# Macaron block on one core: value products of two ticks in one burst, a third buffer of probabilities, bias parts inside the room of y, new plan targets

## The reference, cut to what matters

```python
def ffn(x):                      # on layernormed x
    x_prev = shift_down_by_one_token(x)
    xr = mu_r * x + (1 - mu_r) * x_prev
    xk = mu_k * x + (1 - mu_k) * x_prev
    return sigmoid(xr @ W_r.T) * (square(relu(xk @ W_k.T)) @ W_v.T)

def attn(x):                     # on layernormed x, 16 heads of 16
    q, k, v = split(x @ W_qkv + b_qkv)
    q, k = rope(q), rope(k)
    p = softmax(causal(q @ k.T / 4))
    return (p @ v) @ W_proj + b_proj

x = x + 0.5 * ffn(layernorm(x))
x = x + attn(layernorm(x))
x = x + 0.5 * ffn(layernorm(x))
```

## Time and profile before

| | |
|---|---|
| median of three executions | 3384.6 us |
| profiled execution | 3389.39 us, of which the span 3387.7 us |
| TensorE busy | 3108.6 us (92%) |
| VectorE busy | 2535.7 us (75%) |
| ScalarE busy | 2154.7 us (64%) |
| GpSimd busy | 1488.3 us (44%) |
| mean granted TensorE clock | 0.967 |

### The profile page before, as it was taken

One profiled execution on the slowest core, in us unless ns is written; L12 is line 12 of the kernel. 1 busy time (PEld: TensorE's weight loads), 2 busy tenths in 40 slices (PEclk: granted clock), 3 DMA queues, 4 the chain that ended last, 5 costly groups with the idle time before them and its releaser, 6 DMA issues.

```text
span 3387.7 us, 57478 instructions
## 1 busy us (share of the span) xinstructions
PE 3108.6 (92%) x18368; PEld 1649.0 (49%) x18368; DVE 2535.7 (75%) x8449; ACT 2154.7 (64%) x4737; POOL 1488.3 (44%) x2135
## 2 busy tenths in 40 slices
PE   5689999999899999999999899999999999998997
PEld 4433545545454554545545454554545455454434
DVE  3678888787777877778787777887778787777762
ACT  3266666666666666666666666666666666666663
POOL 5333444454444444454454444444354444444322
PEclk9799999999999999999999999999999999999997
DMA  2334342442433425343442433434343442433321
GB/s 84 49 70 77 67 83 68 76 85 56 91 71 67 87 55 94 67 80 67 76 89 52 92 69 70 82 61 94 62 83 68 76 89 52 89 71 68 70 55 35
DMA packets 201143, 245.36 MB, mean 72 GB/s; under 512 B 67845, under 2 KB 102025, under 8 KB 200841
## 3 DMA queue, kind: packets, MB, share of 16 engines
q1 hardware_dynamic: 200840, 241.69, 36.0%
HBM read 53.35 MB, written 51.38 MB: 31 GB/s over the span
## 4 chain that ended last, share of the span: by engine, by line
PE 66%; DVE 9%; ACT 7%; SPq 6%; DMA 5%; issue 4%; POOL 4%; POOLq 0%; ACTq 0%; DVEq 0%
PE ps_y L597 14%; PE ps_s L575 12%; PE ps_m L582 11%; PE ps_d L654 6%; PE ps_d L648 6%; PE ps_d L642 5%; PE ps_d L645 5%; DMA sw_sb<-qb_sb 4%; DVE ps_m L777 4%; SPq L525 4%; PE ps_d L632 3%; ACT pt_sb L683 3%; PE ps_d L658 2%; PE ps_d L604 2%; DVE ka_sb L801 1%
## 5 line engine op out<-in xcount | busy, mean ns | idle before, releaser
L683 ACT ACTIVATE pt_sb<-ps_s 128x512 f32<-128x512 f32 (+3 forms) x3072 | 1481.5, 494 | 1075.0 <-PE ps_s L575 1058.3
L777 DVE CUSTOM_DVE_ANT_0 ps_m<-ps_m,mask_sb 128x512 f32<-128x512 f32 (+3 forms) x3072 | 1692.5, 568 | 588.8 <-PE ps_m L582 575.7
L582 PE MATMUL ps_m<-kr_sb,qr_sb 96*128 96x512 bf16 (+3 forms) x3072 | 1009.0, 331 | 92.5 <-DVE mx_sb L777 73.6
L575 PE MATMUL ps_s<-qr_sb,kr_sb 99*128 99x512 bf16 (+3 forms) x3072 | 1013.9, 334 | 42.1 <-ACT pt_sb L683 34.8
L902 POOL TENSOR_SCALAR_AFFINE_SELECT pt_sb<-pt_sb 128x512 f32<-128x512 f32 x512 | 343.4, 671 | 949.0 <-ACT pt_sb L683 949.0
L575 PEld LDWEIGHTS ps_s<-qr_sb,kr_sb 99*128 99x128 bf16 x3072 | 299.0, 98 | 838.3 <-issue 324.9
L597 PE MATMUL ps_y<-pt_sb,v_sb 128*32 128x512 f32 (+3 forms) x6144 | 672.7, 510 | 0.0
L777 DVE DVE_READ_ACCUMULATOR2_ANT mx_sb<- 128x1 f32 x3072 | 433.6, 141 | 0.0
L582 PEld LDWEIGHTS ps_m<-kr_sb,qr_sb 96*128 96x128 bf16 x3072 | 300.2, 98 | 215.7 <-DVE mx_sb L777 64.0
L654 PE MATMUL ps_d<-axn_sb,wqk_sb 128*128 128x256 f32 x1024 | 305.5, 392 | 25.2 <-DVE dif_sb L813 23.5
L642 PE MATMUL ps_d<-ka_sb,wk_sb 128*128 128x256 f32 x1024 | 306.0, 396 | 21.7 <-DVE ka_sb L801 20.1
(11 more groups left out here) (74 smaller groups left out, 3215.0 us busy)
## 6 DMA issues: line engine op xcount, KB each, us to landing
kr_sb<-part_sb SPq DMA_DIRECT2D x384, 128.0 KB, 4.5
qr_sb<-part_sb SPq DMA_DIRECT2D x384, 128.0 KB, 4.8
sw_sb<-qb_sb SPq DMA_DIRECT2D x512, 64.0 KB, 2.0
y_way<-yt_sb SPq DMA_DIRECT2D x128, 256.0 KB, 2.2
x_sb<-x SPq DMA_DIRECT2D x64, 256.0 KB, 2.9
yn_sb<-y_way SPq DMA_DIRECT2D x64, 256.0 KB
den_sb<-r_way SPq DMA_DIRECT2D x64, 256.0 KB
out<-x_sb SPq DMA_DIRECT2D x64, 256.0 KB, 2.2
```

Source lines behind the costliest of these rows:

```text
L575: eng.matmul(ps_s[:, slot % NS, 0:width], kr_sb[0:KR + NP, n % RS, j, kb * P:(kb + 1) * P], qr_sb[0:KR + NP, n % RS, j, q0:q0 + width], st ...
L582: eng.matmul(ps_m[:, u % NM, 0:width], qr_sb[0:KR, n % RS, j, i * P:(i + 1) * P], kr_sb[0:KR, n % RS, j, piece * QC:piece * QC + width], s ...
L683: eng.activation(pt_sb[:, tick % 2, j, 0:width], ps_s[:, slot % NS, 0:width], ACT.Exp, scale=SCALE).then_inc(exped, 1)
L777: eng.tensor_tensor_reduce(ps_m[:, u % NM, 0:width], ps_m[:, u % NM, 0:width], mask_sb[:, m0:m0 + width], 1.0, -3e38, ALU.add, ALU.max, mx ...
```

## The change

Five things are edited.

1. `pv` now takes a pair of ticks: first all waits of both ticks, then the 16 MATMUL instructions of both. It runs once in 8 slots, at `slot % 8 == 2` (`PV_AT` 3 becomes 2), for the pair that ended 3 slots before. Before, it ran each 4 slots, for the tick that ended 4 slots before. `pved` counts pairs now, and every wait on it is converted.
2. `pt_sb` has three buffers (`PT = 3`). The third takes 8 KB a partition.
3. `bp_sb` and `bparts_sb` lie inside `yt_sb`; `y_copy` waits once for the bias to be split and sent.
4. The plan's targets. Second feed-forward of batches up to nb-3: base 92 + 25c becomes 70 + 24c. First feed-forward from batch 2 on: -20 + 15c becomes -44 + 18c. Attention's layernorm: 2 + 16c becomes -10 + 18c. `r_QK` of the first pair: 8 + 16c becomes -4 + 18c. `a_V` and `a_bv`: 60 slots behind the layernorm's target becomes 100.
5. With `PV_AT` the y steps' target `done` moves one slot forward.

```diff
--- before.py
+++ after.py
@@ -42,7 +42,8 @@
 NTK = len(TICKS)
 GSLOTS = NTK * G
 BSLOTS = NG * GSLOTS
-PV_AT = 3
+PV_AT = 2
+PT = 3
 MAX_ORDER = [i for k in range(TT // 2) for i in (TT - 1 - k, k)]
 UNITS = [(i, j, piece) for i in MAX_ORDER for j in range(G) for piece in range(i // KQ + 1)]
 NU = len(UNITS)
@@ -86,12 +87,12 @@
                 return at + 160 + 8 * c
             if b == self.nb - 2:
                 return at + BSLOTS + 16 + 24 * c
-            return at + BSLOTS + 92 + 25 * c
+            return at + BSLOTS + 70 + 24 * c
         if b == 0:
             return FIRST + 5 * c
         if b == 1:
             return -60 + 20 * c
-        return at - BSLOTS - 20 + 15 * c
+        return at - BSLOTS - 44 + 18 * c
 
     def describe(self):
         nb, s = self.nb, self.step
@@ -126,7 +127,7 @@
         for b in range(nb):
             for c in range(NCH):
                 i = b * NCH + c
-                t = FIRST + 24 + 6 * c if b == 0 else (b - 1) * BSLOTS + 2 + 16 * c
+                t = FIRST + 24 + 6 * c if b == 0 else (b - 1) * BSLOTS - 10 + 18 * c
                 s("DVE", "a_st0", i, 0.33, t, ("f_xadd", self.ffn_at[b, c, 0], 2), ("a_st1", i - 1, 0))
                 s("DVE", "a_st1", i, 0.51, t, ("a_st0", i, 0), ("a_x1", i - 1, 1))
                 s("POOL", "a_rstd", i, 1.3, t, ("a_st1", i, 3), ("a_x1", i - 1, 1))
@@ -134,15 +135,15 @@
                 s("ACT", "a_x1", i, 0.36, t, ("a_x0", i, 0))
                 s("PE", "a_T", i, 0.5, t, ("a_x1", i, 2))
                 s("ACT", "a_xn", i, 0.48, t, ("a_T", i, 1), ("a_V", i - NCH, 1), ("r_QK", (b - 1) * 2 * NCH + NCH + c, 1))
-                s("PE", "a_V", i, 4, t + 60, ("a_xn", i, 2))
-                s("DVE", "a_bv", i, 0.67, t + 60, ("a_V", i, 1))
+                s("PE", "a_V", i, 4, t + 100, ("a_xn", i, 2))
+                s("DVE", "a_bv", i, 0.67, t + 100, ("a_V", i, 1))
             for pair in range(2):
                 for c in range(NCH):
                     i = (2 * b + pair) * NCH + c
                     if b == 0:
                         t = -40 + 18 * c if pair else FIRST + 32 + 6 * c
                     else:
-                        t = (b - 1) * BSLOTS + (104 + 22 * c if pair else 8 + 16 * c)
+                        t = (b - 1) * BSLOTS + (104 + 22 * c if pair else -4 + 18 * c)
                     s("PE", "r_QK", i, 4, t, ("a_xn", b * NCH + c, 2))
                     s("ACT", "r_b0", i, 0.36, t, ("r_QK", i, 1), ("r_low", i - 2, 1))
                     s("ACT", "r_b1", i, 0.36, t, ("r_b0", i, 0))
@@ -343,11 +344,13 @@
         v_sb = sb("v_sb", [P, 2, TT, H * VW + VPAD])
         qr_sb = sb("qr_sb", [P, RS, G, T], BF16)
         kr_sb = sb("kr_sb", [P, RS, G, T], BF16)
-        pt_sb = sb("pt_sb", [P, 2, G, QC])
+        pt_sb = sb("pt_sb", [P, PT, G, QC])
         yt_sb = sb("yt_sb", [P, NQC, QC])
         den_sb = sb("den_sb", [P, QC])
         dcol_sb = sb("dcol_sb", [P, NQC, G * QC // P])
         yn_sb = sb("yn_sb", [P, NP2, T])
+        bp_sb = yt_sb[0:1, 0, :].rearrange("p (k n) -> p k n", n=C)
+        bparts_sb = yt_sb[0:1, 1, :].bitcast(BF16)[:, 0:NP * C].rearrange("p (k n) -> p k n", n=C)
         mx_sb = sb("mx_sb", [P, 2, 2, G * TT])
         mres_sb = sb("mres_sb", [P, G * TT])
         mp_sb = sb("mp_sb", [P, 2, NP, G * TT], BF16)
@@ -358,8 +361,6 @@
         wqk_sb = sb("wqk_sb", [P, CC, 2 * C])
         wvv_sb = sb("wvv_sb", [P, CC, C])
         wp_sb = sb("wp_sb", [P, NP2, C])
-        bp_sb = sb("bp_sb", [1, 2, C])
-        bparts_sb = sb("bparts_sb", [1, NP, C], BF16)
         brows_sb = sb("brows_sb", [P, C], BF16)
         one_sb = sb("one_sb", [P, P], BF16)
         mur_sb = sb("mur_sb", [P, CC])
@@ -582,20 +583,25 @@
                 eng.matmul(ps_m[:, u % NM, 0:width], qr_sb[0:KR, n % RS, j, i * P:(i + 1) * P],
                            kr_sb[0:KR, n % RS, j, piece * QC:piece * QC + width], start=True, stop=True).then_inc(max_made, 1)
 
-            def pv(tick):
-                n, k, qc, kb, q0, width = tick_of(tick * G)
-                b, g = divmod(n, NG)
-                if DIAGONAL[k]:
-                    pe.wait_ge(selected, selects(tick))
-                else:
-                    pe.wait_ge(exped, G * (tick + 1))
-                pe.wait_ge(*taken_from("a_V", b * NCH + kb // CT))
-                if kb == 0:
-                    pe.wait_ge(y_taken, NQC * n + qc)
-                for j in range(G):
-                    col = (G * g + j) * VW
-                    pv_j = eng.matmul(ps_y[32 * j:32 * j + 32, QC - width:QC], v_sb[:, b % 2, kb, col:col + 32],
-                                      pt_sb[:, tick % 2, j, 0:width], start=(kb == 0), stop=(kb == KQ * (qc + 1) - 1))
+            def pv(pair):
+
+                for tick in (2 * pair, 2 * pair + 1):
+                    n, k = divmod(tick, NTK)
+                    if DIAGONAL[k]:
+                        pe.wait_ge(selected, selects(tick))
+                    else:
+                        pe.wait_ge(exped, G * (tick + 1))
+                    qc, kb = TICKS[k]
+                    pe.wait_ge(*taken_from("a_V", n // NG * NCH + kb // CT))
+                    if kb == 0:
+                        pe.wait_ge(y_taken, NQC * n + qc)
+                for tick in (2 * pair, 2 * pair + 1):
+                    n, k, qc, kb, q0, width = tick_of(tick * G)
+                    b, g = divmod(n, NG)
+                    for j in range(G):
+                        col = (G * g + j) * VW
+                        pv_j = eng.matmul(ps_y[32 * j:32 * j + 32, QC - width:QC], v_sb[:, b % 2, kb, col:col + 32],
+                                          pt_sb[:, tick % PT, j, 0:width], start=(kb == 0), stop=(kb == KQ * (qc + 1) - 1))
                 pv_j.then_inc(pved, 1)
 
             def transposes(dst, src):
@@ -666,8 +672,8 @@
                     dense(name, i, u)
                 if unit_of(slot) is not None:
                     maximum(unit_of(slot))
-                if slot % G == PV_AT and 0 <= slot // G - 1 < n_ticks:
-                    pv(slot // G - 1)
+                if slot % (2 * G) == PV_AT and 0 <= slot // (2 * G) - 1 < n_ticks // 2:
+                    pv(slot // (2 * G) - 1)
 
         @block.scalar
         def _(eng):
@@ -679,8 +685,8 @@
                 n, k, qc, kb, q0, width = tick_of(slot)
                 tick, j = divmod(slot, G)
                 act.wait_ge(scored, slot + 1)
-                act.wait_ge(pved, tick - 1)
-                eng.activation(pt_sb[:, tick % 2, j, 0:width], ps_s[:, slot % NS, 0:width], ACT.Exp, scale=SCALE).then_inc(exped, 1)
+                act.wait_ge(pved, (tick - PT) // 2 + 1)
+                eng.activation(pt_sb[:, tick % PT, j, 0:width], ps_s[:, slot % NS, 0:width], ACT.Exp, scale=SCALE).then_inc(exped, 1)
 
             def dense(name, i):
                 if name in ("f_x0", "f_x1"):
@@ -752,7 +758,9 @@
                     eng.activation(mt_sb[0:rows, i % 2, :], ps_d[:, d, 0:P // 2].bitcast(BF16)[0:rows, :], ACT.Copy).then_inc(taken[d], 1)
                 elif name == "y_copy":
                     n, qc = divmod(i, NQC)
-                    act.wait_ge(pved, n * NTK + sum(KQ * (q + 1) for q in range(qc + 1)))
+                    act.wait_ge(pved, (n * NTK + sum(KQ * (q + 1) for q in range(qc + 1))) // 2)
+                    act.wait_ge(bias_split, 5)
+                    act.wait_ge(bias_rows, 16)
                     act.wait_ge(d_in[qc], 16 * n)
                     act.wait_ge(y_gone[qc], 16 * n)
                     eng.activation(yt_sb[:, qc, :], ps_y[:, :], ACT.Copy).then_inc(y_taken, 1)
@@ -836,7 +844,7 @@
                     b, c = divmod(i, NCH)
                     d = plan.bank["a_V", i]
                     dve.wait_ge(*made_by("a_V", i))
-                    dve.wait_ge(pved, (b - 1) * NG * NTK)
+                    dve.wait_ge(pved, (b - 1) * NG * NTK // 2)
                     for t in range(CT):
                         dst = v_sb[:, b % 2, c * CT + t, 0:H * VW].rearrange("p (h w) -> p h w", w=VW)[:, :, 0:HS]
                         v = eng.tensor_tensor(dst, ps_d[:, d, halves(t)].rearrange("p (h d) -> p h d", d=HS),
@@ -898,7 +906,7 @@
 
             def select(tick):
                 pool.wait_ge(exped, G * (tick + 1))
-                diag = pt_sb[:, tick % 2, :, 0:P]
+                diag = pt_sb[:, tick % PT, :, 0:P]
                 eng.affine_select(out=diag, in_=diag, compare_op=ALU.is_ge, fill=0.0, base=0, pattern=[[0, G], [1, P]],
                                   channel_multiplier=-1).then_inc(selected, 1)
```

## The result

The changed kernel takes 3361.0 us (3356.5 to 3363.4, four runs) against 3386.9 us before. The ratio is 0.992, interval [0.991, 0.994]. It is faster by 26 us, or 0.8%; the prediction was 3246 us, its range 3195 to 3350.

The account below looks back on a forecast made before the run. TensorE, busy 92% of the span, was taken to set the pace. 3389.4 - 69 (burst) - 98 (targets) + 28 (new waits) = 3250 us, or 3246 us against the median of the runs; range 3195 to 3350.

Parts of the forecast that it names:

- Targets: Reordered plan: row-sum DMA finds an empty queue, mid-batch reciprocal stall and half clock go; gain 98 us, ends 0 and 110.
- the stall of the earlier trace: TensorE standing for maxima while VectorE's reciprocal waits for a late row-sum DMA; 65 us, half clock behind it 33 us.
- The burst's saving: Value products: each of 384 pairs loses one way in and out, gains a seam; gain 69 us, ends 81 and 0.
- Third buffer, bias, selects: Extra probabilities buffer, bias in y's room, bursts waiting for selects: each taken at 0; selects up to 16 us.
- The double burst itself: ScalarE stands 0.65 us in a double burst; a third of 128 wide pairs lose it: 28 us, bounds 0 and 250.
- B's second form: Rival at the merged value-product burst: each engine wait takes back what is saved; whole rival 3300 us, chance 0.13.
- C: Rival: double burst starves ScalarE with its two score banks, TensorE stands at scores; slower, 3468 us, chance 0.11.
- A: Rival: the reciprocal's stall on a late DMA stays or finds another place; 3344 us, chance 0.18.

Follow-up runs that it names:

- e2: The kernel before with nothing but the new plan targets, value products still in single bursts: 3274.3 us, ratio 0.966.
- e3: The kernel before with three buffers of probabilities and the bias parts in the room of y, single bursts, old targets: 3390.0 us, ratio 1.000.
- e14: e2 with the plan of the change (computed for value products in slot 2), bursts still single: 3312.1 us, ratio 0.977.
- e11: The change with a pair's two ticks as separate bursts in neighbouring slots, a score between them: 3387.9 us, ratio 0.9995.
- e16: The twin of e9 with the same plan but single bursts, maxima and exponentials over half of the columns: 3194.1 us.
- e9: The change with maxima and exponentials both over half of the columns, the other halves left out: 3194.9 us.

## Why the prediction was wrong

**Targets: right.** The sum had 98 us for the stall of the earlier trace rows and its half clock. e2 measured 116 us with single bursts (with double bursts the same targets are worth more, 3540 - 3361 = 179 us). The cause was as read: the reciprocal's waits at mid-batch are gone, and e2's batch has 9.8 us of waits and 0.3 of clock against 16.1 and 2.5.

**The burst's saving: right, too small.** The sum had 69 us with a seam of 0.03 us. The array saves 91 us; the seam is 2 ns. The row taken as nearest, the seam between the first two passes, was the wrong neighbour: only the first seam of a burst costs 27 ns, and why it differs no run shows. Of the change of tile alone, the Trainium skill, "TensorEngine Tiling (Array Packing)", Key Properties, says that it does not drain the engine. The trace agrees at the later seams, with 2 ns.

**Third buffer, bias, selects: right at nothing.** e3 shows the first two. For the select, after has 0.6 us of idle time ahead of the value products in all.

**The double burst itself: the step that failed.** The sum had 28 us, a third of the wide pairs times ScalarE's idle 0.65 us. Under the change's own plan the new waits are 140 us (3361 - 3312 + 91, e14 being the single version under that plan). I had counted averages over eight slots and one engine's idle time. Two things were missed.

First, the stretch. With bursts four slots apart TensorE goes ahead and is held up in turn; with pairs it makes seven slots with nothing to hold it. The neighbours of the burst, two windows of after, the burst slot and the seven slots behind it (length, then PE, PEld, DVE, ACT, POOL busy, clock, DMA share, GB/s):

```profile
1388.32:1391.14 2.82, 2.82 (x21) 0.90 (x20) 1.95 (x7) 1.73 (x4) 0.00 (x0) 1.00 0.00 0
1391.14:1397.99 6.85, 6.29 (x38) 4.03 (x34) 5.19 (x18) 4.28 (x10) 2.44 (x3) 1.00 0.01 2
```

In the burst slot of 2.82 us ScalarE works 1.73 us and then stands, as its next row in after says:

```profile
1391.57 0.60 ACT L689 ACTIVATE pt_sb<-ps_s 128x512 f32<-128x512 f32 x1 [1.52 <-PE ps_s L576]
```

1.52 us, where I had 0.65. The 0.65 took the burst alone, 1.85 us, less two exponentials; but the dense unit and the maximum stand in the same slot, so that the scores are 2.82 us apart. Over batches 2 to 12 ScalarE stands 1.50 us behind a burst in the mean, and 2.10 where both ticks are wide. That is no more in sum than in e14, where it stands 0.85 and 0.72 us behind two single bursts. It is the same idle time, in one piece.

Over the same batches ScalarE is busy 45% of a burst slot, 73% of the next five and 81% of the two before the burst. In those two VectorE is at 90%. Behind the burst TensorE gets ahead of both, and stands when the stretch ends. Counted by place in the eight slots, from the starts, 13.6 of some 18.6 us of waits a batch in after lie in the last three slots up to the burst (`slot % 8` of 0, 1 and 2); in e14 it is 3.5 of 12.2.

The waits for the two engines themselves are the smaller part. Of e14, against the lines of after above:

```profile
PE ps_s L576 <- ACT pt_sb L684: 22.5, 68, 0.9
PE ps_m L583 <- DVE mx_sb L778: 21.5, 55, 1.9
```

At scores and maxima TensorE waits 32 + 7 = 39 us more in after, at transposes and dense products 56 us more.

e11 against its true base e14 prices the uneven spacing (e11 has the third buffer too, worth nothing in e3): 3388 - 3312 = 76 us. Joining the two bursts on top brings 3361 - 3388 = -27 us where the array saves 91, so joining costs the other 64 us. That the single long gap is what costs them is argued; the odd tick's burst also stands one slot earlier than in e11.

Second, the dense chains. Transposes and feed-forward products wait for steps whose lags the plan counts in slots. Under one plan and with light loads, from e16 to e9, TensorE's waits rise from 5.7 to 10.5 us a batch: at scores from 1.4 to 4.1, at transposes of x from 2.2 to 4.1, at those of maxima from 0.4 to 1.0. Most of the rise at scores is no dense chain: over the whole kernel TensorE waits there 31.7 us for ScalarE's exponentials, against 11.7. The wait for a group's maxima rows, which the plan places, is 17.9 us against 9.8. The place is the same as at full load: 7.5 of e9's waits a batch lie in the last three slots up to the burst, 1.2 of e16's. The slot of a burst now takes 2.28 us in the mean and the seven others 0.74 to 0.98 (in e14 1.72 to 1.80 and 0.69 to 0.84), so four slots of lag can be too short where no burst lies within them. That this unevenness is the cause of what stands at light loads is argued from the plan and these rows; no run isolates it.

**A step that the sum left out.** `PV_AT` in the plan was read as a shift by one slot and cost nothing. It reorders a third of the steps, and costs the single version 38 us (e14), though it spares the merged one 27.

By terms: 3387 - 116 (targets) + 38 (plan at slot 2) - 91 (array) + 76 (spacing) + 64 (joining) = 3358 us, measured 3361. This is bookkeeping and no proof: the last two terms are differences of runs, one of them the change itself, so it has to close. The split also holds only in this order. Under the plan for slot 3 merging costs 114 us and not 49.

**The rivals.** B's second form is nearest: waits took back more than the merging saved, while the targets' gain kept the kernel faster. C's mechanism, TensorE standing at scores because ScalarE ran dry, is a part of it, but C's sign didn't show. TensorE waits 54.3 + 28.9 = 83 us for the exponential and the maximum, against 34.8 + 73.6 = 108 before; only with the stall's 65 us taken out does it rise. A fell. C stood at 0.11 because I weighed it against ScalarE's mean load. "The targets gain, the merging loses" had no case of its own, though the two are separate edits.

The best version run is e2: the new targets with single bursts, 3274 us, 0.966 of before and 0.974 of the change.

## What to carry to other kernels

When several engines share a hand-made rhythm, price a merged burst by what the others do inside it and behind it, not by their mean load: saving 91 us of array time by doubling the burst cost 140 us of waits, although no engine besides TensorE was busy over 76% of the span. Time an edit's parts apart before keeping them together; here one half was worth 116 us and hid the other's loss, and the parts' effects didn't add up to the whole's. And a constant that a scheduler reads is a change of the whole order, not of one target.

## What the hardware showed that was not expected

Value products on 32-column strips cost 97 ns to enter from full-width products and 118 ns to leave, the same within 2 ns in every kernel run. Within the burst only the first change of pass costs 27 ns; each later one, to another tick's weights too, costs 2 ns. The same step list in a plan that differs in 1928 slots moved the time by +38 us in one kernel and -27 us in the other, so where an edit also reorders the steps, a difference of 1% can't be put down to the edit until a run holds the order fixed.
